# Eighteen late steps behind the last slots instead of twelve, the late halves' additions among them, the last half summed in a bank of its own

## The chip, the cores and the metric

The kernel runs on one core of a Trainium2 chip. The metric is the device time of one execution in microseconds (us), taken as the median of a few runs. PE is TensorE (matmuls), ACT is ScalarE, DVE is VectorE, POOL is GpSimd and SP is SyncE, which here only issues DMAs. Each engine works through its own instructions in order and waits on semaphores for the others.

## What is computed

8192 tokens (16 sequences of 512) with 128 features, all in float32. First a block per sequence: layer norms, a time mix with a scan along the sequence, a channel mix. Then a layer with one expert out of 16 for each token and a shared expert for all:

```python
x = x + attn(layernorm(x))                # time mix (scan) and channel mix
hidden = layernorm(x).reshape(-1, 128)
logits = hidden @ router_w.T              # 16 experts, the best one is taken
routed_out = einsum(up * silu(gate), down_proj)      # of the token's expert, EF = 128
shared = (silu(hidden @ shared_gate_w.T) * (hidden @ shared_up_w.T)) @ shared_down_w.T   # SF = 512
out = x + shared + expert_sum
```

## The kernel before

The program has two parts. In 23 rounds (`ROUNDS`) the 16 sequences run through the first block in a software pipeline; each token's row (its features for the expert, its own number, and the sum so far) is then scattered to a place in DRAM (`sorted_rows`) where the tokens of one expert lie together. The second part takes these sorted rows in 80 slots of 128 tokens, two slots (a pair) at a time: 40 pairs (`NP`), in 43 turns (`TURNS`). `one_turn(m)` stands in the program of each engine. In turn m

- SP has loaded pair k long before, from `sorted_rows` into a ring of 12 buffers (L392), once the scatter of pair k-12 is done
- PE transposes the features of pairs m and m+1 when m is even (L691), and DVE copies them out (L1133)
- PE does the down products of pair m-3 (L697) and the gate and up products of pair m-1 (L704, L705)
- ACT copies the weights of the two slots' experts (L865) and takes Silu of the gate product (L870); DVE multiplies it with the up product (L1141) and adds the down product to the rows (L1136)
- POOL scatters the two slots' rows to `out` (L1287), each token to its own place

The shared expert is not finished for all tokens in the first part. A sequence has two halves of 256 tokens; 16 halves are late (`LATE`, units u = 0 to 15). Units 0 to 2 are worked out in the last rounds, the others (`FIRST_LATE` = 3 and up) in late steps put between the slots. A unit has four steps. Steps 0 and 1 are its gate and up products (`unit_product`, L418: 4 matmuls, 8 records in the profile), ACT's Silu (L735) and DVE's product (L1124). Steps 2 and 3 are its down products (`unit_down_late`, L426: 4 matmuls, 8 records each) into bank 0 (`ACC`), which ACT copies out to `sh_of(u)` after step 3 (L738). `late_order` weaves two units: (u, 0), (u-1, 2), (u, 1), (u-1, 3). All gate products of the second part but the first two go to bank 2 and all up products to bank 3, so a gate product waits for the Silu before it and an up product for DVE's product before it; a down step waits for ACT's copy of the unit before.

`late_steps(m)` says which late steps stand in turn m: one each in turns 0 and 1, then 34 spread over turns 4 to 39 (`LATE_TURN` = 4), and the last 12 (`LATE_AFTER`) in the three turns that have no new pair: one in turn 40, one in turn 41 and the other ten in turn 42.

When all scatters are done (`all_stored`), SP and POOL load the late halves' rows back from `out` in 8 DMAs of two units each (`load_late`, L330; the places are `SP_LOADS` = 0, 2, 6, 8, 12, 14 and `GP_LOADS` = 4, 10). DVE then adds `sh_of(u)` to each unit (L1152), after all its other work, and the units are stored: 0 to 11 by SP, 12 to 15 (`ACT_STORES` = 4) by ACT, each when `tl_add` has counted it (`store_late`, L336).

Of the kernel before, what the change touches and what calls it, by code (L numbers as in the profile page):

```python
# [23 lines left out]
ALU = mybir.AluOpType  # L24
# [11 lines left out]
NT = NTOK // T  # L36
HALF = T // 2
# [55 lines left out]
def program(nc, x, w_main, w_exp, vecs, out):  # L93
# [4 lines left out]
    with ExitStack() as ctx:  # L98
# [124 lines left out]
        ACT_STORES = 4  # L223
        SP_LOADS, GP_LOADS = [u for u in range(0, N_LATE, 2) if u % 6 != 4], [u for u in range(0, N_LATE, 2) if u % 6 == 4]
        HALF_TILE = 10
# [3 lines left out]
        FIRST_LATE = len(C_TILES)  # L229
        STEPS_BEFORE, LATE_TURN, LATE_AFTER = 4, 4, 12  # L230
        GU_BEHIND, DN_BEHIND = 1, 3
# [65 lines left out]
        def stores(k):  # L297

            return range(2) if k < NP - 1 else range(1)

        def late_act(u):
            return actB if u % 2 else actC
# [7 lines left out]
        def tl_sem(u):  # L310

            if u - u % 2 in GP_LOADS:
                return "tl_in", 16 * (len(GP_LOADS) - 1)
            return f"xr_in{u // 2}", 32 * laps(u // 2)
# [85 lines left out]
        def _(pe):  # L400
# [52 lines left out]
            def late_step(u, step):  # L453
# [16 lines left out]
                else:  # L470
                    if u == FIRST_LATE:
                        wait(pe, "cbase", NT)
                    wait(pe, "lac", u, step - 1)
                    wait(pe, "lsh", u - 1)
                    unit_down_late(ACC, late_act(u)[step - 2], step - 2).then_inc(s["lD"], 1)

# [238 lines left out]
        def _(act_e):  # L715
# [12 lines left out]
            def late_step(u, step):  # L728
                if step < 2:
# [5 lines left out]
                    af(late_sg(u)[step][:, :], late_bank(u, step)[0][:, :], ACT.Silu).then_inc(s["lsg"], 1)  # L735
                elif step == 3:
                    wait(act_e, "lD", u)
                    af(sh_of(u), ACC[:, 0:HALF], ACT.Copy).then_inc(s["lsh"], 1)  # L738
# [141 lines left out]
        def _(dve):  # L880
# [235 lines left out]
            def late_step(u, step):  # L1116
                if step < 2:
# [6 lines left out]
                    v.tensor_tensor(late_act(u)[step][:, :], late_sg(u)[step][:, :], late_bank(u, step)[1][:, :], ALU.mult).then_inc(s["lac"], 1)  # L1124

            for u, step in late_order()[:STEPS_BEFORE]:
                late_step(u, step)

            def one_turn(m):
# [12 lines left out]
                for u, step in late_steps(m):  # L1142
                    late_step(u, step)

            for m in range(TURNS):
                one_turn(m)
            for u in range(N_LATE):
                if u % 2 == 0:
                    dve.wait_ge(s[tl_sem(u)[0]], tl_sem(u)[1] + 16)
                wait(dve, "cbase", NT)  # L1150
                wait(dve, "lsh", u)
                v.tensor_tensor(tl_of(u), tl_of(u), sh_of(u), ALU.add).then_inc(s["tl_add"], 1)  # L1152

# [179 lines left out]
```

## Time and profile before

| | |
|---|---|
| median of 3 timed runs | 510.09 us (509.06 to 510.21) |
| span of the profiled execution, first to last instruction | 528.1 us |
| TensorE busy | 497.9 us (94%) |
| VectorE busy | 363.4 us (69%) |
| ScalarE busy | 345.9 us (66%) |
| GpSimd busy | 347.9 us (66%) |
| the second part's first scatter | at 380.20 us |
| late halves' loads are issued | from 513.08 us |
| last late step's matmuls end | at 521.35 us |
| last addition ends | at 524.72 us |

All times of the trace are from the profiled execution, whose span is longer than the timed runs; of the profiled execution no other time is recorded than this span. Times in a row are microseconds from the start of the span, unless marked ns. PE's rows are records: one float32 matmul leaves two. Buffers are named by the tile they were made as: the slots use buffers of the first part again, so `er`, `e`, `num` and others in a row are their names there. The names `xn1tok`, `xn1T`, `ew` and `kr` in a row of L738 or L1152 are the late units 0 to 3, 4 to 7, 8 to 11 and 12 to 15 (`sh_of`).

### The profile page before, as it was taken

Reading aid. Unit: us, or ns where it says so; the run is one execution under the profiler, and the core shown is the slowest. Engines: PE = TensorE matmul, PEld = TensorE weight load, DVE = VectorE, ACT = ScalarE, POOL = GpSimd, SP = SyncE. Lnnn points to the kernel's source line nnn. Section 1 sums busy time; section 2 is a strip of 40 time slices with the busy share of each in tenths; the row PEclk is TensorE's granted clock in tenths of the full one; section 3 lists DMA queues with packets and bytes.
Section 4 is the critical chain, followed back from the end, with each engine's and each line's share of the span. In section 5 each row is a group of like instructions: output and inputs, shape, how many; then the busy total and the mean of one; then the engine's idle time right before and its main releaser. Section 6 shows DMA issues by size and latency. Waiting matters only on the chain.

```text
span 528.1 us, 10518 instructions
## 1 busy us (share of the span) xinstructions
PE 497.9 (94%) x3101; PEld 406.0 (77%) x3101; DVE 363.4 (69%) x1036; ACT 345.9 (66%) x643; POOL 347.9 (66%) x576
## 2 busy tenths in 40 slices
PE   8889999999999999999999999999998998799984
PEld 7646777877877877878577679888887987799874
DVE  5978889889889889888787888446434433444335
ACT  3777897987987988977789775632534534455321
POOL 6766668778778778785887866635154565556660
PEclk9999999999999999999999999999999899999988
DMA  6015001101101101101010010102877434441009
GB/s 219 2 51 209 20 21 41 60 22 41 60 21 42 60 22 42 50 11 62 12 50 21 21 41 32 41 21 72 204 207 189 137 101 125 129 116 49 30 12 308
DMA packets 33031, 39.32 MB, mean 74 GB/s; under 512 B 4913, under 2 KB 29113, under 8 KB 32720
## 3 DMA queue, kind: packets, MB, share of 16 engines
q1 hardware_dynamic: 26640, 24.97, 16.2%
q0 software_dynamic: 5760, 13.16, 7.2%
q8 instruction: 26, 0.43, 0.3%
q10 hardware_dynamic: 576, 0.52, 0.3%
q14 instruction: 29, 0.24, 0.2%
HBM read 21.68 MB, written 17.93 MB: 75 GB/s over the span
## 4 chain that ended last, share of the span: by engine, by line
PE 61%; DVE 7%; ACT 7%; issue 7%; another core or an unknown queue 7%; POOL 6%; DMA 2%; SPq 1%; ACTq 0%; DVEq 0%; POOLq 0%
PE bank L418 14%; PE bank L411 8%; PE bank L435 4%; PE bank L405 3%; PE bank L426 3%; PE bank L704 2%; PE bank L705 2%; PE bank L534 2%; PE bank L520 2%; PE bank L544 2%; PE bank L530 2%; PE bank L525 2%; PE bank L551 2%; PE bank L577 2%
## 5 line engine op out<-in xcount | busy, mean ns | idle before, releaser
L418 PE MATMUL bank<-hT,wm 128*128 128x256 f32 x512 | 128.7, 390 | 3.4 <-ACT hT L821 2.2
L418 PEld LDWEIGHTS bank<-hT,wm 128*128 128x128 f32 x512 | 94.0, 195 | 21.8 <-ACT hT L821 7.2
L1287 POOL DMA_INDIRECT out<-shared x55 | 53.9, 979 | 47.3 <-DVE shared L1136 32.2
L411 PEld LDWEIGHTS bank<-wm,k 128*128 128x128 f32 x512 | 62.3, 192 | 10.7 <-issue 6.9
L411 PE MATMUL bank<-wm,k 128*128 128x128 f32 x512 | 63.7, 277 | 1.2 <-ACT k L838 0.9
L870 ACT ACTIVATE er<-bank 128x256 f32<-128x256 f32 x40 | 15.2, 383 | 54.9 <-remote 33.1
L1141 DVE TENSOR_TENSOR e<-er,bank 128x256 f32<-128x256 f32 x40 | 16.8, 420 | 31.1 <-ACT er L870 20.3
L1287 POOL DMA_INDIRECT out<-rows x24 | 23.5, 978 | 20.5 <-DVE rows L1136 11.3
L799 ACT ACTIVATE h<-rows,smE 128x128 f32<-128x128 f32 x64 | 26.3, 482 | 12.6 <-POOL smE L1231 12.5
L435 PE MATMUL bank<-wm,actA 128*128 128x128 f32 x240 | 32.8, 280 | 0.0
L435 PEld LDWEIGHTS bank<-wm,actA 128*128 128x128 f32 x240 | 29.3, 192 | 0.2
L1245 POOL TENSOR_SCALAR shared<-shared,smA 128x128 f32<-128x128 f32 x64 | 27.8, 445 | 0.0
L761 ACT ACTIVATE xn1tok<-shared,smA 128x128 f32<-128x128 f32 x62 | 25.4, 482 | 3.2 <-POOL smA L1199 3.2
L1207 POOL TENSOR_TENSOR smA<-smA,half 128x8 f32<-128x8 f32 x15 | 25.7, 1716 | 1.2
L766 ACT ACTIVATE xn2T<-bank,vec 128x512 f32<-128x512 f32 x16 | 12.4, 777 | 20.4 <-PE bank L405 20.2
L1222 POOL TENSOR_SCALAR rows<-h,sc 128x128 f32<-128x128 f32 x64 | 24.1, 393 | 1.6
L1182 POOL TENSOR_SCALAR smC<-mvC 128x4 f32<-128x4 f32 x16 | 3.9, 244 | 30.8 <-DVE mvC L901 30.8
L896 DVE BATCH_NORM_STATS2 stA<-shared 128x6 f32<-128x128 f32 x64 | 13.9, 279 | 14.2 <-DMA shared<-x 14.2
L1258 POOL DMA_INDIRECT sorted_rows<-rows,posi x16 | 18.7, 1170 | 7.4 <-DVE posi L973 3.9
L534 PEld LDWEIGHTS bank<-wm,xn2T 128*128 128x128 f32 x128 | 16.8, 192 | 7.6 <-issue 7.6
L1264 POOL DMA_INDIRECT sorted_rows<-rows,posi x16 | 18.0, 1123 | 4.9 <-issue 4.9
L426 PE MATMUL bank<-wm,den 128*128 128x128 f32 x144 | 20.3, 289 | 0.5 <-issue 0.5
(258 smaller groups left out, 1401.6 us busy)
## 6 DMA issues: line engine op xcount, KB each, us to landing
shared<-sorted_rows SPq DMA_DIRECT2D x56, 128.5 KB
shared<-x SPq DMA_DIRECT2D x16, 256.0 KB
rows<-sorted_rows SPq DMA_DIRECT2D x24, 128.5 KB
wexp<-w_exp SPq DMA_DIRECT2D x2, 1536.0 KB, 9.6
sorted_rows<-filler SPq DMA_DIRECT2D x17, 128.5 KB
shared<-out SPq DMA_DIRECT2D x6, 256.0 KB
out<-shared SPq DMA_DIRECT2D x12, 128.0 KB, 2.3
sorted_rows<-rows,posi POOLq DMA_INDIRECT x64
```

The lines of the kernel that those rows point to most:

```text
L411: ins = mm(grp(acc, g), grp(lhs, g), W(name, f), start=(f == 0 and g == 0), stop=(f == F // P - 1), skip_group_check=True)
L418: ins = mm(dst[:, j * HALF:(j + 1) * HALF], W(name, 2 * pair_ + j), src[:, half * HALF:(half + 1) * HALF], start=True, stop=True)
L426: ins = mm(grp(acc, g), lhs[:, j * HALF + g:(j + 1) * HALF:2], W("down", 2 * pair_ + j), start=(pair_ == 0 and j == 0 and g == 0), stop=(p ...
L435: ins = mm(grp(acc, 2 * half + g), lhs[:, at_:at_ + P], W("down", 2 * pair_ + j), start=(pair_ == 0 and j == 0 and g == 0), stop=(pair_ == ...
L534: ins = mm(grp(REC_B, g), grp(xn2T[t % 2], g), W("Wrec"), start=True, stop=True)
L761: ins = af(grp(xn1tok[t % 2], g), grp(xin[t % XR], g), ACT.Identity, bias=smA[t % 3][:, 5, g:g + 1], scale=smA[t % 3][:, 4, g:g + 1])
L799: ins = af(grp(h[t % 2], g), base_of(t)[:, g, :], ACT.Identity, bias=smE[t % 3][:, 3, g:g + 1], scale=smE[t % 3][:, 1, g:g + 1])
L1207: g_.tensor_tensor(sm[:, 3:5, :], sm[:, 1:3, :], half8[:, :, :], ALU.pow).then_inc(s["pA"], 1)
L1222: ins = g_.tensor_scalar(rows[t % 3][:, g, 0:D], grp(h[t % 2], g), sc[t % 2][:, g:g + 1], 1.0, ALU.mult, ALU.mult)
L1245: ins = g_.tensor_scalar(grp(xn0[t % 4], g), grp(xin[t % XR], g), smA[t % 3][:, 0, g:g + 1], smA[t % 3][:, 3, g:g + 1], ALU.add, ALU.mult)
L1258: g_.indirect_dma_start(sorted_ap, bass.IndirectOffsetOnAxis(posi[t % 3][:, 2:3].bitcast(U32), 0), rows[t % 3][:, 2, :], None).then_inc(s[ ...
L1287: g_.indirect_dma_start(out, bass.IndirectOffsetOnAxis(xr[k % RING][:, j, D:D + 1].bitcast(U32), 0), xr[k % RING][:, j, D + 1:ROW], None, ...
```

## The change

Six more late steps are taken from the turns with slots and put into turn 42 (`LATE_AFTER` 18 instead of 12): 28 instead of 34 are spread over turns 4 to 39. The additions of units 0 to 13 are moved between DVE's last late products: units 0 to 3 behind the product of (14, 1), 4 to 7 behind (15, 0), 8 to 13 behind (15, 1). The last unit's down products go to bank 6 (`late_sum`), which the slots' transposes used; ACT does not copy them, and DVE adds the bank directly. SP loads pairs 0, 2, 4, 6, 8, 14 and POOL 10, 12.

```diff
--- before.py
+++ after.py
@@ -221,13 +221,14 @@
 
         TAB_ROWS = 15
         ACT_STORES = 4
-        SP_LOADS, GP_LOADS = [u for u in range(0, N_LATE, 2) if u % 6 != 4], [u for u in range(0, N_LATE, 2) if u % 6 == 4]
+        SP_LOADS, GP_LOADS = [0, 2, 4, 6, 8, 14], [10, 12]
+        ADDED_BEHIND = {(N_LATE - 2, 1): range(0, 4), (N_LATE - 1, 0): range(4, 8), (N_LATE - 1, 1): range(8, N_LATE - 2)}
         HALF_TILE = 10
         WARM_FIRST, WARM_BEFORE, WARM_BEHIND = 20, (8, 12), 4
         FULL_SLOTS = NTOK // P - NE
         FILL_PAIRS = range(4, 4 + NE)
         FIRST_LATE = len(C_TILES)
-        STEPS_BEFORE, LATE_TURN, LATE_AFTER = 4, 4, 12
+        STEPS_BEFORE, LATE_TURN, LATE_AFTER = 4, 4, 18
         GU_BEHIND, DN_BEHIND = 1, 3
         W_BEHIND = GU_BEHIND - 1
         TURNS = NP + DN_BEHIND
@@ -298,6 +299,10 @@
 
             return range(2) if k < NP - 1 else range(1)
 
+        def late_sum(u):
+
+            return bank[6] if u == N_LATE - 1 else ACC
+
         def late_act(u):
             return actB if u % 2 else actC
 
@@ -309,7 +314,7 @@
 
         def tl_sem(u):
 
-            if u - u % 2 in GP_LOADS:
+            if u // 2 * 2 in GP_LOADS:
                 return "tl_in", 16 * (len(GP_LOADS) - 1)
             return f"xr_in{u // 2}", 32 * laps(u // 2)
 
@@ -471,8 +476,11 @@
                     if u == FIRST_LATE:
                         wait(pe, "cbase", NT)
                     wait(pe, "lac", u, step - 1)
-                    wait(pe, "lsh", u - 1)
-                    unit_down_late(ACC, late_act(u)[step - 2], step - 2).then_inc(s["lD"], 1)
+                    if u == N_LATE - 1:
+                        wait(pe, "xhT", NP // 2 - 1)
+                    else:
+                        wait(pe, "lsh", u - 1)
+                    unit_down_late(late_sum(u), late_act(u)[step - 2], step - 2).then_inc(s["lD"], 1)
 
             def one_round(n):
                 at = at_round(n)
@@ -733,7 +741,7 @@
                         wait(act_e, f"cac{step}", NT)
                         wait(act_e, f"hac{step}", NT)
                     af(late_sg(u)[step][:, :], late_bank(u, step)[0][:, :], ACT.Silu).then_inc(s["lsg"], 1)
-                elif step == 3:
+                elif step == 3 and u < N_LATE - 1:
                     wait(act_e, "lD", u)
                     af(sh_of(u), ACC[:, 0:HALF], ACT.Copy).then_inc(s["lsh"], 1)
 
@@ -1123,6 +1131,18 @@
                         wait(dve, f"hD{step}", NT)
                     v.tensor_tensor(late_act(u)[step][:, :], late_sg(u)[step][:, :], late_bank(u, step)[1][:, :], ALU.mult).then_inc(s["lac"], 1)
 
+            def add_late(units):
+                for u in units:
+                    if u % 2 == 0:
+                        dve.wait_ge(s[tl_sem(u)[0]], tl_sem(u)[1] + 16)
+                    if u == N_LATE - 1:
+                        wait(dve, "lD", u)
+                        v.tensor_tensor(tl_of(u), tl_of(u), late_sum(u)[:, 0:HALF], ALU.add).then_inc(s["tl_add"], 1)
+                    else:
+                        wait(dve, "cbase", NT)
+                        wait(dve, "lsh", u)
+                        v.tensor_tensor(tl_of(u), tl_of(u), sh_of(u), ALU.add).then_inc(s["tl_add"], 1)
+
             for u, step in late_order()[:STEPS_BEFORE]:
                 late_step(u, step)
 
@@ -1141,15 +1161,11 @@
                     v.tensor_tensor(xact[k % 4][:, :], xsg[k % 2][:, :], XGU_B[k % 2][:, 2 * P:4 * P], ALU.mult).then_inc(s["xact"], 1)
                 for u, step in late_steps(m):
                     late_step(u, step)
+                    add_late(ADDED_BEHIND.get((u, step), ()))
 
             for m in range(TURNS):
                 one_turn(m)
-            for u in range(N_LATE):
-                if u % 2 == 0:
-                    dve.wait_ge(s[tl_sem(u)[0]], tl_sem(u)[1] + 16)
-                wait(dve, "cbase", NT)
-                wait(dve, "lsh", u)
-                v.tensor_tensor(tl_of(u), tl_of(u), sh_of(u), ALU.add).then_inc(s["tl_add"], 1)
+            add_late(range(N_LATE - 2, N_LATE))
 
 
         @block.gpsimd
```

PE, from turn 39 to the first steps of turn 42, before. L697 are down products of slots, L704 and L705 their gate and up products, L418 and L426 the late steps of the two kinds:

```order
L697 MATMUL bank<-an,e 128x128 x2
...
L697 MATMUL bank<-xn2T,e 128x128 x2
L704 MATMUL bank<-num,rv 128x128
L705 MATMUL bank<-num,rv 128x128
L418 MATMUL bank<-hT,wm 128x256 x4
L697 MATMUL bank<-th,e 128x128 x2
L426 MATMUL bank<-wm,den 128x128 x4
L697 MATMUL bank<-rv,e 128x128
L418 MATMUL bank<-hT,wm 128x256 x4
L426 MATMUL bank<-wm,actB 128x128 x4
```

The same place now (L705 is the down product of slots, L712 and L713 gate and up, L423 and L431 the late steps), with the start of what follows:

```order
L705 MATMUL bank<-an,e 128x128 x2
...
L705 MATMUL bank<-xn2T,e 128x128 x2
L712 MATMUL bank<-num,rv 128x128
L713 MATMUL bank<-num,rv 128x128
L423 MATMUL bank<-hT,wm 128x256 x4
L705 MATMUL bank<-th,e 128x128 x2
L431 MATMUL bank<-wm,actB 128x128 x4
L705 MATMUL bank<-rv,e 128x128
L423 MATMUL bank<-hT,wm 128x256 x4
L431 MATMUL bank<-wm,actB 128x128 x4
L423 MATMUL bank<-hT,wm 128x256 x4
L431 MATMUL bank<-wm,den 128x128 x4
```

The turns read alike, but behind the last slot's down product (`rv,e` with a single matmul) stand 16 late steps now, where ten stood.

DVE behind the last slots, before. L1136 adds a slot pair's down product, L1124 is a late product, L1152 an addition to the late halves:

```order
L1136 TENSOR_TENSOR shared<-bank,shared 128x2x128 x2
L1124 TENSOR_TENSOR den<-ev,bank 128x512 x2
L1124 TENSOR_TENSOR actB<-sgB,bank 128x512 x2
L1152 TENSOR_TENSOR shared<-shared,xn1tok 128x256 x4
L1152 TENSOR_TENSOR shared<-shared,xn1T 128x256 x4
L1152 TENSOR_TENSOR shared<-shared,ew 128x256 x4
L1152 TENSOR_TENSOR shared<-shared,kr 128x256 x4
```

And now (L1132 is a late product, L1144 an addition, L1140 the addition that reads the bank):

```order
L1132 TENSOR_TENSOR den<-ev,bank 128x512
L1132 TENSOR_TENSOR actB<-sgB,bank 128x512 x2
L1132 TENSOR_TENSOR den<-ev,bank 128x512 x2
L1144 TENSOR_TENSOR shared<-shared,xn1tok 128x256 x4
L1132 TENSOR_TENSOR actB<-sgB,bank 128x512
L1144 TENSOR_TENSOR shared<-shared,xn1T 128x256 x4
L1132 TENSOR_TENSOR actB<-sgB,bank 128x512
L1144 TENSOR_TENSOR shared<-shared,ew 128x256 x4
L1144 TENSOR_TENSOR shared<-shared,kr 128x256 x3
L1140 TENSOR_TENSOR shared<-shared,bank 128x256
```

Eight additions stand ahead of the last late product, and eight behind it.

## Rows read from the trace of the kernel before

**Rows 1.** The page's first line: span of the profiled execution.
```profile
span 528.1 us, 10518 instructions
```
**Rows 2.** Windows of 4 us: busy times, granted clock, DMA share, GB/s.
```profile
504.00:508.00 4.00, 4.00 (x19) 3.65 (x18) 1.62 (x4) 0.38 (x1) 3.08 (x4) 0.57 0.02 0
...
520.00:524.00 4.00, 1.34 (x12) 1.15 (x10) 3.40 (x11) 0.38 (x1) 0.00 (x0) 1.00 1.03 349
```
**Rows 3.** Chain of waits, an undisturbed stretch: start, duration, what.
```profile
476.40 0.44 PE bank L691 x4
...
478.18 0.94 PE bank L426 x8
...
480.46 1.73 PE bank L418 x8
482.19 0.44 PE bank L691 x4
```
**Rows 4.** The chain's unrecorded waits: first and last of eight.
```profile
390.21 5.46 another core or an unknown queue
...
498.15 4.59 another core or an unknown queue
```
**Rows 5.** Timeline of POOL: start, duration, operation, idle time before it and releaser.
```profile
440.87 0.98 POOL L1287 DMA_INDIRECT out<-shared  x1 [3.03 <-DVE shared L1136]
442.15 0.98 POOL L1287 DMA_INDIRECT out<-shared  x1 [0.30 <-issue]
...
450.68 0.98 POOL L1287 DMA_INDIRECT out<-rows  x1 [2.41 <-DVE rows L1136]
```
**Rows 6.** Timelines of PE: turn 4's transposes, and turns 39 to 42.
```profile
379.36 0.38 PE L691 MATMUL bank<-ident,shared 128*128 128x128 f32 x2
...
497.55 0.61 PE L697 MATMUL bank<-an,e 128*128 128x128 f32 x4
...
498.89 0.61 PE L697 MATMUL bank<-xn2T,e 128*128 128x128 f32 x4
...
503.65 0.71 PE L697 MATMUL bank<-th,e 128*128 128x128 f32 x4 [1.97 <-DVE e L1141]
504.20 1.73 PE L426 MATMUL bank<-wm,den 128*128 128x128 f32 x8
505.72 0.64 PE L697 MATMUL bank<-rv,e 128*128 128x128 f32 x2
```
**Rows 7.** Timeline of all engines behind the last slot.
```profile
506.15 2.73 PE L418 MATMUL bank<-hT,wm 128*128 128x256 f32 x8
...
508.72 1.10 PE L426 MATMUL bank<-wm,actB 128*128 128x128 f32 x8
...
513.08 3.15 SPq L330 DMA_DIRECT2D shared<-out  x6
...
513.92 1.13 PE L418 MATMUL bank<-hT,wm 128*128 128x256 f32 x4 [0.47 <-DVE den L1124]
...
517.81 0.69 DVE L1124 TENSOR_TENSOR actB<-sgB,bank 128x512 f32<-128x512 f32 x1 [1.98 <-PE bank L418]
518.42 1.43 DVE L1152 TENSOR_TENSOR shared<-shared,xn1tok 128x256 f32<-128x256 f32 x4
...
519.22 2.12 PE L426 MATMUL bank<-wm,actB 128*128 128x128 f32 x16 [0.56 <-ACT kr L738]
520.60 1.43 DVE L1152 TENSOR_TENSOR shared<-shared,xn1T 128x256 f32<-128x256 f32 x4 [0.75 <-DMA shared<-out]
...
523.29 1.43 DVE L1152 TENSOR_TENSOR shared<-shared,kr 128x256 f32<-128x256 f32 x4
```
**Rows 8.** Stores by source line (ns; starts), groups by line, DMA issues (landing).
```profile
L336 ACTq DMA_DIRECT2D out<-shared x4: 412/461/591, 523.7 to 525.2; - x4
...
L1136 DVE TENSOR_TENSOR shared<-bank,shared 128x256 f32<-128x256 f32 x26 | 10.9, 419 | 10.8 <-PE bank L697 5.5 <-remote 4.9 <-issue 0.3
...
shared<-out POOLq DMA_DIRECT2D x2, 256.0 KB, 5.6
```

## The prediction

> **What bounds the kernel now.** I read the page's first line and set it beside the times [rows 1]: the profiled execution's span is 528.1 us, the median of the timed runs 510.09 us, so the profiled execution is 18.0 us or more behind a timed one, and the reader has to ask where. The change lies in the last quarter, so next came the chain of waits. In an undisturbed stretch [rows 3] it is TensorE (PE) alone: from one x4 transpose to the next, two turns, are 476.40 to 482.19 = 5.79 us. Those two turns hold 0.44 us of transposes, twice 1.34 of down, gate and up products (the step from one down product to the next in a turn without a late step, 497.55 to 498.89 in [rows 6]) and two late steps, 0.94 and 1.73: 5.79 us, with nothing between them. So a turn costs PE 1.56 us for its pair of slots and 2.90 us with a late step (1.34 on average). GpSimd (POOL) issues the two scatters of a turn 1.28 us apart [rows 5], 2.57 us a turn, so it is not the bound.
>
> The same chain has eight pieces that end in no recorded work [rows 4], 35.8 us together, the first at 390.21, the last from 498.15 to 502.74. In each, VectorE (DVE) and ScalarE (ACT) stand still although PE's records say that their product is done. From the transposes of turn 4 at 379.36 to the last slot's down product at 505.72 [rows 6] are 126.4 us. The work in it is 38 turns x 1.56 = 59.3 and 36 late steps x 1.34 = 48.1, together 107.4 us: 19.0 us are lost. That is nearly the 18.0 us by which the profiled execution is long. I conclude that most of this loss belongs to the profiled execution and that in a timed run the slots go at PE's pace. This is an inference from two numbers, and the main rival hangs on it.
>
> The Trainium skill, page "Runtime: NRT & Kernel Launch", section "The ~15µs preamble/postamble breakdown", puts 9 to 15 us around a kernel's own instructions; by it a timed run's span would be 495 to 501 us and the surplus of the profiled one 27 to 33 us. No row here shows that part. It would make the slots of a timed run still more surely PE's, with the same sum.
>
> Behind the slots [rows 6, 7] PE does ten late steps, 506.15 to 521.35 us. Their work is 4 x 1.73 + 6 x 0.94 = 12.6 us; the rest is a stretch at the lower clock [rows 2] and two gaps of 0.47 and 0.56 us. DVE, which has to do all 16 additions after its last product at 517.81, starts them at 518.42 and ends at 524.72. The last store leaves at 525.2 and the span ends 2.9 us later [rows 7, 8]. So what ends the kernel is DVE's block of additions and not PE, which is done 3.4 us before it.
>
> **The change, part by part.**
>
> Six late steps leave the slots, three of each kind (34 between turns 4 and 39 become 28): 3 x 1.73 + 3 x 0.94 = 8.0 us of PE. Where the turns are PE's, the last slot is done 8.0 us sooner: 36 turns at 1.56 + 28 x 1.34 / 36 = 2.60 us on average instead of 1.56 + 34 x 1.34 / 36 = 2.83. Bounds of what is given back: 8.0 us, and 0. A turn without a late step stands in the trace, from the down product at 497.55 to the next at 498.89 [rows 6]: 1.34 us, what the undisturbed stretch holds too, no gap. So I take 8.0 us.
>
> The same six steps are added behind the last slot: +8.0 us of PE. One bank pair (2 and 3) takes all gate and up products there, so a stall can sit between steps. Before, two gaps did, 0.47 us before 513.92 and 0.56 us before 519.22 [rows 7]. Per six steps I add 0.5 us, the first gap once; bounds 0 and 1.5.
>
> The last half sums in bank 6. The second gap is PE waiting for ACT to empty bank 0 (the releaser in the row at 519.22); with its own bank the last unit needs only DVE's product, done at 518.50, and starts behind the step before it, at 518.66. PE ends 0.56 us sooner, at 520.8 on the old clock. ACT's last copy (0.38 us) goes; the addition reads the bank itself, at the price of an addition with a bank operand, 0.42 us [rows 8].
>
> Of the additions, units 0 to 3 go behind the product of (14, 1), 4 to 7 behind (15, 0), 8 to 13 behind (15, 1). Four take 1.43 us and one 0.42, so each starts (1.43 - 0.42) / 3 = 0.34 us after the one before [rows 7, 8]. Four of them with a product are 0.69 + 1.43 = 2.1 us, and PE needs 0.94 + 1.73 = 2.67 us until its next up product: they fit, 0.5 us to spare. Behind the last product remain eight instead of 16: from 518.42 the six end at 520.5, unit 14 at 520.9, and unit 15, which waits for PE at 520.8, at 521.25, where 524.72 stood. ACT's stores of units 12 to 15 go out from 520.25 at one every 0.5 us, the last at 521.8 instead of 525.2. So the end comes 3.4 us sooner in the profiled execution. Of that, 0.75 us is DVE's wait for a load [rows 7], which a timed run, whose scatters lag less behind, may not have: for the timed run I take 3.0 (2.6 to 3.5).
>
> What the moved additions wait for: in order on DVE, the product of (15, 0) and with it PE's up product of (15, 1) are queued behind the landing of pairs 0 and 2. Before, loads were issued 7.4 us after the last slot's down product (505.72 to 513.08), and the slowest took 5.6 us to land [rows 6 to 8]: 13.0 us. Now (14, 1) ends five gate and four down steps after that point, 5 x 1.73 + 4 x 0.94 = 12.4 us and the gaps; pairs 0 and 2 are the first two of SP's queue and land before the slowest. Pairs 4 and 6 are wanted 2.7 us later, 8 to 13 another 2.7 us later. SP takes pair 4 from POOL and gives it 12; each issue is 0.46 us. All that is covered, narrowly for the first two in the worst case.
>
> Traffic: loads and stores are 4.2 MB. Before, they ran at 349 GB/s from 520 to 524 us, the DMA engines busy throughout [rows 2]; at that rate 4.2 MB are 12 us. Now the loads have 12 us to themselves and only 1 MB of stores is left for the last 3 us.
>
> Sum on the profiled execution: -8.0 + 8.0 + 0.5 - 3.4 = -2.9, a span of 525.2 us. On a timed run: -8.0 + 8.0 + 0.5 - 3.0 = -2.5, so **507.6 us**.
>
> **The rivals.**
>
> A, slower: the slots are not PE's in a timed run. If the eight unrecorded waits are real there and come at a pace that PE's work does not set (the scatters go in sixes, and the next six starts about 10 us after, 440.87 and 450.68 [rows 5]), fewer steps in a turn only lengthen them. Then up to 8.0 us is not given back: 510.09 + 8.0 + 0.5 - 3.0 = 515.6. It decides where less than 8.0 - 2.5 = 5.5 us of the 8.0 are given back. For it: eight such waits. Against: 19.0 against 18.0 us. 17 in 100; it may be partial, about 511.5.
>
> B, no change: 1 to 4 us of the 8.0 are lost. POOL's 79 scatter intervals need 79 x 1.28 = 101.3 us, and PE's slots would fall to 107.4 - 8.0 = 99.4 us: POOL becomes as slow as PE. That delays the loads, not PE, as long as the ring of 12 pairs does not fill. 509 to 510.5 us, 13 in 100.
>
> C, the lower clock behind the slots. The row: from 504 to 508 us the granted clock was 0.57, that is 1.2 GHz for most of it and 2.4 after, behind 1.97 us without a matmul [rows 2, 6]; the down step from 504.20 took 1.52 us to the next product instead of 0.94, the gate and up step from 506.15 to 508.72 2.57 instead of 1.73 [rows 3, 6, 7]: +1.4 us. More of PE's work now stands in that place and depends on ACT and DVE step by step. Once more gives 507.6 + 1.4 = 509.0 us, 7 in 100. The Trainium skill, page "TensorE: Matmul & The Clock Gate", section "HAM oscillation — how this bites in real kernels", has idle stretches between bursts return the array to the lower clock; by that rule this would come with every such gap. The gap of 0.56 us before 519.22 was followed by no fall (granted clock 1.00 from 520 to 524 [rows 2]), so the trace bears it out for the long gap only.
>
> D, the additions hold DVE back: pairs 0 and 2 land after (14, 1). Each us late is a us on the end; 0.5 to 2 us, 508 to 509.6. Against: 12.4 us of steps before they are wanted. 5 in 100, mostly no change.
>
> E, more: no stall behind the slots, the 3.4 us of the profile whole, and a second effect of less work per turn: 505.0 to 506.6, 10 in 100.
>
> **How the numbers follow.** The forecast (507.6, itself 506.6 to 508.6) has 48 in 100, E 10. With the parts of C and D below 508.56 that makes faster 0.62. Within 0.3% (about 1.5 us, what a measurement of this kernel can tell from no change) is 0.20: B, most of C and D, and the light part of A. Slower is 0.18: A with what is left. The range of 8 in 10 runs from E's lower end, 505.0, to the partial case of A, 511.5.
>
> **What would show it.** In the changed profile: two slot turns without an unrecorded wait near 5.2 us on average; 16 late steps in 20.6 us of work and at most 1.5 us of gaps after the last slot's down product; additions between the products with no DVE wait for a load before them; the last one, from bank 6, right behind PE's last matmul, and the span's end 3.3 us after it where it was 6.75 us. It would be wrong if the last slot's down product does not come about 8 us sooner in the profile, or if products of (15, 0) and (15, 1) start later than 1 us behind their up products.

## The result and the profile after

The changed kernel took **503.95 us** (median of 6 runs, 503.52 to 507.69), the kernel before 509.97 us beside it (6 runs, 509.06 to 510.48). The ratio is 0.9888, with an interval of 0.9862 to 0.9913: 6.0 us faster, where 2.5 were forecast. The sign was right, the size was not, and 503.95 lies 1 us under the range of 505.0 to 511.5.

The page of the changed kernel, its span and its busy times:

```profile
span 504.8 us, 10516 instructions
...
PE 488.0 (97%) x3101; PEld 400.4 (79%) x3101; DVE 363.0 (72%) x1036; ACT 348.6 (69%) x642; POOL 348.9 (69%) x576
```

[rows 1] had 528.1 us in that place, 18 us over the timed median. The profiled execution of the changed kernel took 506.53 us, 1.7 us more than its span. So a profiled execution is not long as such, and the first question was what the 528.1 us had been.

The timeline of the changed kernel, PE behind and around the last slot (start, duration, operation), and SP's loads:

```profile
480.48 0.39 PE L705 MATMUL bank<-rv,e 128*128 128x128 f32 x2
480.70 1.89 PE L423 MATMUL bank<-hT,wm 128*128 128x256 f32 x8
...
487.71 3.15 SPq L335 DMA_DIRECT2D shared<-out  x6
...
499.34 2.05 PE L431 MATMUL bank<-wm,actB 128*128 128x128 f32 x16
```

The last slot's down product starts at 480.48, the transposes of turn 4 at 382.44: the slots take 98.0 us. PE's last matmul ends at 499.34 + 2.05 = 501.39, 20.9 us behind the last down product. From there to the span's end are 3.4 us.

The timeline of DVE and of ACT's stores in the changed kernel, with the idle time before each and its releaser:

```profile
493.34 0.69 DVE L1132 TENSOR_TENSOR den<-ev,bank 128x512 f32<-128x512 f32 x1 [1.97 <-PE bank L423]
493.94 1.42 DVE L1144 TENSOR_TENSOR shared<-shared,xn1tok 128x256 f32<-128x256 f32 x4
...
496.61 1.42 DVE L1144 TENSOR_TENSOR shared<-shared,xn1T 128x256 f32<-128x256 f32 x4
...
499.27 1.42 DVE L1144 TENSOR_TENSOR shared<-shared,ew 128x256 f32<-128x256 f32 x4
500.61 1.08 DVE L1144 TENSOR_TENSOR shared<-shared,kr 128x256 f32<-128x256 f32 x3
501.06 1.89 ACTq L341 DMA_DIRECT2D out<-shared  x4
501.62 0.41 DVE L1140 TENSOR_TENSOR shared<-shared,bank 128x256 f32<-128x256 f32 x1
```

No addition waits for a load, and the last one, from bank 6, starts 0.23 us behind PE's last matmul. All this is close to what the prediction drew. What it got wrong is therefore looked for in the kernel before, against which the change is set.

### The profile page after: what moved, and what is told of

The parts are those of the page before. It is cut to its first block and busy times, and to the rows that moved or that the text cites. A ratio compares the mean times of both kernels' runs of the same rounds, so it can differ in the third digit from the quotient of the medians.

```text
span 504.8 us, 10516 instructions
## 1 busy us (share of the span) xinstructions
PE 488.0 (97%) x3101; PEld 400.4 (79%) x3101; DVE 363.0 (72%) x1036; ACT 348.6 (69%) x642; POOL 348.9 (69%) x576
## 5 line engine op out<-in xcount | busy, mean ns | idle before, releaser
L423 PE MATMUL bank<-hT,wm 128*128 128x256 f32 x512 | 125.5, 384 | 4.6 <-ACT hT L829 4.4
L423 PEld LDWEIGHTS bank<-hT,wm 128*128 128x128 f32 x512 | 91.6, 190 | 22.5 <-ACT hT L829 10.5
L1274 POOL DMA_INDIRECT sorted_rows<-rows,posi x16 | 18.7, 1170 | 7.4 <-DVE posi L981 3.1
L985 DVE TENSOR_TENSOR ew<-bank,ew 128x512 f32<-128x512 f32 x16 | 11.0, 687 | 17.8 <-ACT ew L815 11.6
L904 DVE BATCH_NORM_STATS2 stA<-shared 128x6 f32<-128x128 f32 x64 | 13.9, 280 | 12.4 <-DMA shared<-x 12.4
L774 ACT ACTIVATE xn2T<-bank,vec 128x512 f32<-128x512 f32 x16 | 12.4, 778 | 14.3 <-PE bank L410 14.0
L1132 DVE TENSOR_TENSOR actB<-sgB,bank 128x512 f32<-128x512 f32 x14 | 9.6, 688 | 15.2 <-PE bank L423 11.5
```

Of the source, the lines that this page charges most:

```text
L423: ins = mm(dst[:, j * HALF:(j + 1) * HALF], W(name, 2 * pair_ + j), src[:, half * HALF:(half + 1) * HALF], start=True, stop=True)
L1274: g_.indirect_dma_start(sorted_ap, bass.IndirectOffsetOnAxis(posi[t % 3][:, 2:3].bitcast(U32), 0), rows[t % 3][:, 2, :], None).then_inc(s[ ...
```

## Experiments

Three theories. **P**: the slots lose 2 to 4 us in ordinary runs too, and a lighter turn wins them back. **Q**: the slots are PE's; the end of the kernel before costs more in ordinary runs than the first profile showed. **R**, formed after the second group: that end hangs on the scatters, the loads behind them and the stores, and not on PE. Each comparison below is with the kernel before on the same chip, with its interval of 95%.

### First group: a chip on which the kernel before takes 532 us

The kernel before, unchanged:

> The kernel before, unchanged, profiled once more. What is open: the change gained 6.0 us where 2.5 were forecast, while the changed kernel's profile shows the tail as forecast (3.4 us from TensorE's last matmul to the end). Theory P: in ordinary runs too the kernel before loses 2 to 4 us in its slots, to waits that end in no recorded work or to gaps of TensorE, and the change takes them away. Then this profile has a span near 508.3 us (the time less 1.7) and shows such waits, and its tail is the known 6.0 to 6.8 us behind TensorE's last matmul. Theory Q: the slots lose nothing in ordinary runs; the tail behind the last slot costs more there than in the first profile. Then TensorE is without a gap up to the last slot, and the tail is 9 us or more.

The kernel before with one number changed:

```diff
-STEPS_BEFORE, LATE_TURN, LATE_AFTER = 4, 4, 12
+STEPS_BEFORE, LATE_TURN, LATE_AFTER = 4, 4, 18
```

> The kernel before with one number changed: 18 late steps behind the last slots instead of 12. Additions all at the end, the last unit in bank 0, as before. P: the slots give back more than the 8.0 us moved, so this alone gains 2 to 4 us, 506 to 508 us. Q: 8.0 us out and 8.0 us in, with another 0 to 0.5 us of gaps: 510.0 to 510.5 us.

The changed kernel with `LATE_AFTER` back at 12, which leaves the early additions and the own bank:

> The changed kernel with 12 late steps behind the slots instead of 18: the additions between the products and the own bank alone. Now the product of (14, 1) comes some 5.3 us after the last slot's down product and the loads of pairs 0 and 2 land 8 to 10 us after it, so VectorE waits for them 3 to 5 us ahead of the product of (15, 0) and holds TensorE. P and Q alike: 3.4 us gained on the additions, 3 to 5 lost, 509.5 to 512 us. Under Q a gain larger than 3.4 us on the tail may show, 507 to 509 us.

The changed kernel with all of the additions but the last two behind the last product:

```diff
-ADDED_BEHIND = {(N_LATE - 2, 1): range(0, 4), (N_LATE - 1, 0): range(4, 8), (N_LATE - 1, 1): range(8, N_LATE - 2)}
+ADDED_BEHIND = {(N_LATE - 1, 1): range(0, N_LATE - 2)}
```

> The changed kernel with the additions of units 0 to 7 moved back behind the last late product: 18 steps, own bank and the new order of loads kept. Eight more additions of 0.34 us on VectorE's tail, 2.7 us: 503.95 + 2.7 = 506.7 us under both theories. If P is right, this lies 3 us below the kernel before for the move of the six steps; under Q it would have to be the early additions that bring the gain, and this would be 508 us or more.

Measured: the kernel before 532.0 us here (the median of all its runs on this chip is 532.33); the move alone 539.98, ratio 1.0155 (1.0102 to 1.0209); additions and bank with 12 steps 531.14, 0.9978 (0.9944 to 1.0013); additions at the end 538.18, 1.0108 (1.0069 to 1.0147). No theory had foreseen 532 us, and none of the expectations for the three edits came true: the timed runs here are as long as the first profile, and the move alone, for which 506 to 510.5 us were expected, is 7.7 us slower than before. Windows of 40 us in the slots (PE, PEld, DVE, ACT and POOL busy with their counts, granted clock, DMA share, GB/s), of the kernel before on this chip:

```profile
425.00:465.00 40.00, 34.76 (x232) 31.57 (x231) 14.82 (x32) 16.59 (x41) 22.20 (x24) 0.91 0.41 113
```

and of the kernel before on another chip (the profile of the second group, below):

```profile
425.00:465.00 40.00, 40.00 (x312) 38.54 (x311) 20.50 (x43) 22.44 (x55) 27.63 (x29) 1.00 0.49 138
```

The same stretch holds 232 of PE's matmuls against 312. The chain of waits of the long run shows where, in the same kind of piece as [rows 4]:

```profile
401.96 6.56 another core or an unknown queue
...
444.99 6.95 another core or an unknown queue
```

From the trace's semaphore events one can work out how long after the end of its record each of PE's updates in the slots arrives (the next update of that semaphore). In the first profile and in the six traces taken on the two chips of 532 and 535 us it is 2.4 to 2.8 us on average, over 1 us for 74 to 92 of 138 to 147; in the nine others it is 0.01 to 0.08 us, over 1 us for at most 2. (Some updates are missing from the long traces, so these averages are rough.) So on such a chip, a lagging one in what follows, the next engine gets PE's word late. Since the ends of PE's records are modelled, this does not tell whether the matmuls end late or only the update comes late. In all seven lagging traces the first update that is over 0.5 us late belongs to a matmul some 4 us behind the first indirect scatter of the program, and the last one within 3 us of the start of the last scatter; no run tested whether the scatters cause it.

The slots take 124.9 us in the kernel before and 129.5 with the move alone: six steps fewer in them, and nothing given back. That is rival A's mechanism. It can't be what made the change faster in the first comparison, so the same had to be asked on a chip without it.

### Second group: a chip on which the kernel before takes 510 us

The kernel before:

> The kernel before, unchanged, once more, on whatever chip this is. On the chip of the last four runs it took 532 us, and TensorE's semaphore updates came up to some microseconds behind its records in the slots. Where the chip takes 510 us for it: theory P says that 2 to 3 us of such lag are in the slots there too (more than 107.4 us from turn 4's transposes to the last slot's down product), theory Q that the slots take 106 to 107.5 us and the tail more than the 21 us of the first profile.

The changed kernel:

> The changed kernel, unchanged, beside the kernel before on this chip. If the chip is one where the kernel before takes 532 us, the six steps moved cost 8 us and the additions and the bank give 5 to 6 back: 2 to 4 us slower than before. If it is one where before takes 510 us: 504 us, as in the first comparison.

The move alone, with the edit of the first group:

> The kernel before with 18 late steps behind the slots, nothing else. On a chip with the lag: 8 us slower, as measured. On one without: P (the slots give back more than 8.0 us) 2 to 4 us faster than before; Q (they give back 8.0) within 0.5 us of before.

The changed kernel with the last half summed in bank 0 again, emptied by ACT:

```diff
-            return bank[6] if u == N_LATE - 1 else ACC
+            return ACC
...
-                    if u == N_LATE - 1:
-                        wait(pe, "xhT", NP // 2 - 1)
-                    else:
-                        wait(pe, "lsh", u - 1)
+                    wait(pe, "lsh", u - 1)
...
-                elif step == 3 and u < N_LATE - 1:
+                elif step == 3:
```

Its addition then reads the copy in SBUF, as the other fifteen do.

> The changed kernel with the last unit back in bank 0 and ScalarE's copy of it back, all else kept. Then the last down products wait for ScalarE's copy of unit 14, 0.56 us, and the last addition for another copy, 0.4 to 0.5 us: 0.9 to 1.1 us behind the changed kernel under both theories, on either kind of chip.

Measured: before 510.29 (0.9993, 0.9975 to 1.0011); the change 503.12 (0.9878, 0.9820 to 0.9935); the move alone 507.23, ratio 0.9934 (0.9910 to 0.9959), some 3 us; without the own bank 504.24, 504.38 and 505.40 us, ratio 0.9871 (0.9827 to 0.9915), which can't be told from the whole change by its times (a fourth run of it took 1293.72 us, for which nothing here gives a reason; it is left out). The move alone was expected within 0.5 us of before by Q and 2 to 4 us faster by P, so its time speaks for P; its stages do not. The stages of the traces, in us (the slots from turn 4's transposes to the last slot's down product; PE's tail from there to the end of its last matmul; the rest to the span's end):

| kernel | slots | PE's tail | rest | span |
|---|---|---|---|---|
| before, first profile | 126.4 | 15.6 | 6.8 | 528.1 |
| before, this chip | 106.1 | 13.7 | 9.3 | 509.0 |
| the change, first profile | 98.0 | 20.9 | 3.4 | 504.8 |
| the change, this chip | 98.1 | 20.9 | 3.4 | 500.8 |
| move alone | 98.6 | 21.7 | 6.3 | 506.4 |
| without the own bank | 98.7 | 21.7 | 3.7 | 503.7 |

The parts in front of the slots differ by up to 1.6 us between two traces of the same kernel, so the stages say more than the spans. The slots give back 8.0 us of 8.0 with the change and 7.5 with the move alone, none more than was moved: **P falls**. The tail takes 7.2 with the change and 8.0 with the move alone. The rest of 9.3 us in the kernel before is the surprise, 2.5 us more than in the first profile; the move alone makes it 3.0 us shorter, the change 5.9. The timeline of the kernel before on this chip, from the last slot on:

```profile
486.05 0.39 PE L697 MATMUL bank<-rv,e 128*128 128x128 f32 x2
...
491.04 0.98 POOL L1287 DMA_INDIRECT out<-shared  x1 [0.30 <-issue]
...
493.23 3.15 SPq L330 DMA_DIRECT2D shared<-out  x6
493.79 1.55 POOL L330 DMA_DIRECT2D shared<-out  x2 [1.77 <-DMA out<-shared]
...
496.25 0.69 DVE L1124 TENSOR_TENSOR actB<-sgB,bank 128x512 f32<-128x512 f32 x1 [1.97 <-PE bank L418]
496.86 1.43 DVE L1152 TENSOR_TENSOR shared<-shared,xn1tok 128x256 f32<-128x256 f32 x4
497.65 2.12 PE L426 MATMUL bank<-wm,actB 128*128 128x128 f32 x16 [0.56 <-ACT kr L738]
...
500.93 1.43 DVE L1152 TENSOR_TENSOR shared<-shared,xn1T 128x256 f32<-128x256 f32 x4 [2.65 <-DMA shared<-out]
502.28 1.42 DVE L1152 TENSOR_TENSOR shared<-shared,ew 128x256 f32<-128x256 f32 x4
503.62 1.43 DVE L1152 TENSOR_TENSOR shared<-shared,kr 128x256 f32<-128x256 f32 x4
504.07 2.08 ACTq L336 DMA_DIRECT2D out<-shared  x4
```

DVE stands 2.65 us before the second four additions, for POOL's loads; in [rows 7] it was 0.75. Both of POOL's loads count one semaphore (`tl_in`), and the addition of unit 4 waits for both: by the semaphore's updates pair 4 was there at 499.62 and pair 10 at 500.91, where the wait ends. A semaphore for each would have won little, since SP's pair 6, needed two additions later, came at 501.11. The loads leave at 493.23, 7.2 us after the last slot's down product (7.4 in the first profile), since the last scatter starts 5.0 us after it. But PE is done sooner: its tail is 13.7 us here against 15.6. So the loads are late for the additions. Their landing, by the DMA issues (count, KB each, median us):

```profile
shared<-out SPq DMA_DIRECT2D x6, 256.0 KB, 7.1
shared<-out POOLq DMA_DIRECT2D x2, 256.0 KB, 6.1
```

and the DMA engines' share (the last column but one) is full all the while:

```profile
496.00:500.00 4.00, 3.21 (x25) 2.86 (x23) 2.03 (x5) 0.57 (x2) 0.00 (x0) 1.00 0.90 283
500.00:504.00 4.00, 0.00 (x0) 0.00 (x0) 3.07 (x10) 0.20 (x1) 0.00 (x0) 1.00 1.01 348
504.00:508.00 4.00, 0.00 (x0) 0.00 (x0) 1.05 (x4) 0.00 (x0) 0.00 (x0) 0.60 0.88 294
```

From 493.2 to the end, 4.2 MB of loads and stores have to pass: that is theory R, tested in the third group.

The Trainium skill, page "DMA: Bandwidth & Descriptors", section "🔬 Latency and other measured facts", gives HBM's access 2 us at high load as the main part of a transfer's fixed cost. The 7.1 us here are mostly something else: the eight loads of 256 KB share full engines, and the same loads with a quarter of the bytes (below) landed 2.6 us after their issue. Reckoning with the page's figure alone would have had the additions never wait.

### Third group: what the end hangs on, on another such chip

The kernel before with loads of a quarter of the bytes:

```diff
-                eng.dma_start(shared[:, u * HALF:(u + 2) * HALF].rearrange("p (h c) -> p h c", h=2),
-                              halves_[:, a0:a1 + 1:a1 - a0, :]).then_inc(s[tl_sem(u)[0]], 16)
+                eng.dma_start(shared[:, u * HALF:(u + 2) * HALF].rearrange("p (h c) -> p h c", h=2)[:, :, 0:HALF // 4],
+                              halves_[:, a0:a1 + 1:a1 - a0, 0:HALF // 4]).then_inc(s[tl_sem(u)[0]], 16)
```

> The kernel before, but each late half's load brings a quarter of its columns (64 of 256), so that three quarters of the late halves' output is not the reference's; additions, stores and all else are kept. In the kernel before on an undisturbed chip the additions wait 2.65 us for a load, TensorE ends 9.27 us before the end, and the DMA engines are busy from the last scatter to the end. Theory R: there the end hangs on the scatters, the loads behind them and the stores, not on TensorE. Then this kernel loses the wait: additions from 0.6 us behind the last late product in one row, TensorE's end to the end 6.3 us, 507.3 us. Rival: the wait hides nothing and the end is where it was, 510 us. On a chip with the lag (532 us): 530 to 532 us.

The early additions and the own bank with 12 late steps behind, again:

> The changed kernel with 12 late steps behind the slots, for an undisturbed chip. The loads go out 7.1 us after the last slot's down product, the product of (14, 1) ends 5.5 us after it. R: VectorE waits for pairs 0 and 2, which land 3 to 4 us after their issue, so the product of (15, 0) is some 4 to 5 us late and TensorE's end with it, but the end hangs on the DMA traffic anyway: 13 us from the loads' issue, so 507 to 509.5 us. If the end hung on TensorE alone: 510.3 + 4.5 - 5.9 = 509 us, so only the trace tells these apart: under R the stores' DMA is busy to the end.

The changed kernel with `LATE_AFTER` at 24:

> The changed kernel with 24 late steps behind the slots instead of 18. With the loads landed well before the additions want them, nothing more is to be had: 503.1 us, within 0.5. TensorE's slots would be 90.5 us where GpSimd's 79 scatter intervals need 101.3, so GpSimd lags 10 us more; if that holds TensorE through the ring of 12, 504 to 506 us. On a chip with the lag: another 8 us slower.

The kernel before with pair 4 first on SP's queue and 12 on POOL's:

```diff
-SP_LOADS, GP_LOADS = [u for u in range(0, N_LATE, 2) if u % 6 != 4], [u for u in range(0, N_LATE, 2) if u % 6 == 4]
+SP_LOADS, GP_LOADS = [0, 2, 4, 6, 8, 14], [10, 12]
```

> The kernel before with the changed kernel's order of loads alone: pairs 0, 2, 4, 6, 8, 14 by SyncE, 10 and 12 by GpSimd. If what ends the kernel before is its additions waiting for pair 4 and 10 on GpSimd's queue, the wait of 2.65 us falls to 0 to 1 us and this gains 2 to 2.5 us, 508 us. If it is the 4.2 MB behind the last scatter (13 us at 320 GB/s), the order gives 0 to 1 us, 509.5 us.

Measured, beside 511.17 us for the kernel before:

| kernel | us | ratio (interval) | slots | PE's tail | rest |
|---|---|---|---|---|---|
| quarter loads | 507.52 | 0.9935 (0.9910 to 0.9961) | 106.3 | 13.7 | 6.3 |
| additions and bank, 12 steps | 510.39 | 0.9995 (0.9976 to 1.0013) | 105.8 | 18.6 | 4.6 |
| the change with 24 steps | 503.95 | 0.9863 (0.9839 to 0.9886) | 90.5 | 28.9 | 3.4 |
| order of the loads | 510.80 | 0.9989 (0.9973 to 1.0005) | 106.0 | 13.7 | 9.9 |

**Quarter loads.** Nothing but the loads' bytes is cut, and 3.65 us go, close to R's 507.3, with the rest at 6.3 us, just where the move alone has it. DVE's additions run through:

```profile
496.68 1.42 DVE L1152 TENSOR_TENSOR shared<-shared,xn1tok 128x256 f32<-128x256 f32 x4
498.02 1.42 DVE L1152 TENSOR_TENSOR shared<-shared,xn1T 128x256 f32<-128x256 f32 x4
```

The same two rows with the move alone, where six more steps stand behind the slots and the additions are as before:

```profile
497.21 1.42 DVE L1152 TENSOR_TENSOR shared<-shared,xn1tok 128x256 f32<-128x256 f32 x4
498.55 1.42 DVE L1152 TENSOR_TENSOR shared<-shared,xn1T 128x256 f32<-128x256 f32 x4
```

Two unlike edits take the same wait away and win some 3 us each, so R holds on chips without the lag. This is what the six moved steps are worth: from the start of the last scatter to the first addition are 13.8 us with the move alone and 5.8 before.

**Order of the loads.** The wait isn't POOL's queue being behind: with pair 4 third on SP's, it landed 7.6 us after its issue, DVE waited longer, and the time did not change. The loads share the DMA engines, and another place in the queues did not bring this one in sooner.

```profile
502.06 1.50 DVE L1152 TENSOR_TENSOR shared<-shared,xn1T 128x256 f32<-128x256 f32 x4 [3.48 <-DMA shared<-out]
```

**Additions and bank with 12 steps.** This is rival D's mechanism in full. The timeline of DVE and PE:

```profile
495.93 1.52 DVE L1144 TENSOR_TENSOR shared<-shared,xn1tok 128x256 f32<-128x256 f32 x4 [4.39 <-DMA shared<-out]
497.37 0.68 DVE L1132 TENSOR_TENSOR actB<-sgB,bank 128x512 f32<-128x512 f32 x1
...
498.20 1.14 PE L423 MATMUL bank<-hT,wm 128*128 128x256 f32 x4 [2.97 <-DVE actB L1132]
499.13 1.91 PE L431 MATMUL bank<-wm,den 128*128 128x128 f32 x8
...
501.30 1.43 DVE L1144 TENSOR_TENSOR shared<-shared,xn1T 128x256 f32<-128x256 f32 x4 [3.25 <-DMA shared<-out]
```

DVE waits 4.39 us for the loads with PE's next input queued behind, and PE stands 2.97 us. The tail is 4.9 us longer than before, the rest 4.7 us shorter: nothing won, where R had let expect 507 to 509.5 us. The early additions pay only once the move has made time for the loads.

It also shows rival C's price. Windows of the same kernel:

```profile
498.00:502.00 4.00, 3.80 (x18) 3.74 (x19) 0.75 (x4) 0.39 (x1) 0.00 (x0) 0.64 0.93 302
```

After the 2.97 us without a matmul the granted clock is 0.64 in this window, mostly 1.2 GHz where it had been 2.4, and the down step of eight matmuls at 499.13 took 1.91 us instead of 1.10. After the 0.56 us gap of the kernel before, the window 496 to 500 above has 1.00. The Trainium skill, page "TensorE: Matmul & The Clock Gate", section "HAM oscillation — how this bites in real kernels", has waits for a DMA between bursts of matmuls bring the lower clock back. The trace agrees for the gap of 2.97 us, behind which stands DVE's wait for a load; the gap of 0.56 us, a wait for ACT's copy, had no such effect.

**24 steps.** Twelve steps moved instead of six: 503.95 us, ratio 0.9863 against 0.9878 for the change in the second group, intervals that overlap; 503.1 within 0.5 had been expected. The slots give back another 7.6 us and the tail takes 8.0. So POOL's scatters do not bound slots of 98 us (rival B), and once the loads are ahead more room for them brings nothing.

### Fourth group: a lagging chip again

The changed kernel with the additions at the end, and the changed kernel:

> The changed kernel with the additions of units 0 to 7 moved back behind the last late product; 18 steps, own bank and order of loads kept. On an undisturbed chip the loads have landed before the first addition, so only eight additions of 0.34 us are added to the tail: 2.7 us behind the changed kernel, 505.9 us, 4.4 us faster than before. On a chip with the lag of TensorE's semaphore updates: again 1% slower than before.

> The changed kernel unchanged on one more chip. Undisturbed (before 510 to 511 us): 503 to 504 us. With the lag (before 530 us or more): the steps moved cost 8 us, as the move alone did (7.7), and the tail gives back 2.7 us for the early additions more than the kernel with all additions at the end, which was 5.9 us slower than before: 3 us slower than before.

Measured beside 535.0 us for the kernel before: 542.0, ratio 1.0147 (1.0067 to 1.0227), and 537.45, ratio 1.0040 (1.0008 to 1.0071). On such a chip the change is **slower**, by some 2 us, where 3 had been expected. The stages of the lagging traces, with the time of the traced run:

| kernel | run | slots | PE's tail | rest |
|---|---|---|---|---|
| before, first profile | not recorded | 126.4 | 15.6 | 6.8 |
| before | 535.6 | 124.9 | 21.0 | 6.3 |
| additions and bank, 12 steps | 529.9 | 121.7 | 21.9 | 4.3 |
| move alone | 540.8 | 129.5 | 21.7 | 6.3 |
| additions at the end, first group | 540.1 | 126.5 | 24.9 | 7.1 |
| additions at the end, this group | 540.8 | 127.4 | 23.6 | 7.1 |
| the change | 542.5 | 128.3 | 28.8 | 3.4 |

With 34 late steps the slots took 121.7 to 126.4 us, with 28 of them 126.5 to 129.5: no trace shows any of the 8.0 us given back, and the slots are 3.6 us longer on average. The granted clock is not the main thing missing. In the window below, of the move alone on the first lagging chip, it is 1.00, and yet 244 matmuls are done where the same kernel does 313 on a chip without the lag:

```profile
425.00:465.00 40.00, 33.14 (x244) 29.95 (x243) 15.80 (x34) 17.65 (x44) 22.93 (x24) 1.00 0.41 120
```

The early additions shorten the rest from 7.1 to 3.4 us here. The medians of the last two kernels are 4.5 us apart, with intervals wide enough for the 2.7 that was expected. The change's trace is of its longest run, 5 us over its median, so its tail of 28.8 us says little of the others.

## Why the prediction was wrong

**The surplus of 18 us** was taken for something that profiled executions add. In kind that was wrong: it belongs to the chip on which that profile was taken, or to one like it; on two chips the timed runs are that long too. The first profile's updates lag like those of the long runs. The conclusion that was drawn from it, that on the chips of 510 us the slots go at PE's pace, was right, but not for its reason: the same kernel on a lagging chip loses about as much in timed runs too, and that the change was timed on a chip without the lag was luck.

**−8.0 in the slots.** Right: 106.1 to 98.1 us, where 107.4 to 99.4 were forecast. In the changed kernel's windows of the slots PE is busy without a pause:

```profile
420.00:440.00 20.00, 20.00 (x158) 19.33 (x157) 10.36 (x23) 12.28 (x29) 15.19 (x16) 1.00 0.52 151
```

**+8.0 behind them.** Right: the move alone has a tail of 21.7 us against 13.7.

**+0.5 of gaps.** Did not come: those 8.0 us are the steps themselves. The stall at 513.92 in [rows 7] is not in the tail of a chip without the lag, and neither is the lower clock. Step by step the first profile's tail loses 0.84 us at that stall (0.47 of them the gap) and 1.05 to the clock; 15.6 less these is 13.7. (The prediction's 1.4 us for the clock holds 0.58 from before the tail.)

**−0.56 from the own bank.** Right in kind and near in size: PE's tail is 20.9 us with it and 21.7 without, and the rest 3.4 against 3.7, together 1.1 us by one pair of traces.

**−3.0 for the additions: the step that failed.** The prediction had 3.4 us in the profile, took off up to 0.75 for DVE's wait for a load "which a timed run, whose scatters lag less behind, may not have", and so took 3.0. It is the other way round. The loads are issued just as late (7.2 us after the last down product, 7.4 in the first profile), while PE's tail, the thing that covers them, is 1.9 us shorter, and the wait is 1.9 us longer: 2.65 us. That tail could have been reckoned from the prediction's own rows, since the gap of 0.47 us and the lower clock stood in them as effects of the waits.

The 3.0 counts to the end of the kernel and holds the 0.56 of the own bank. Measured in the same way the term is 6.7 us: 0.8 from the tail, 5.9 from the rest (9.3 to 3.4). The move alone brings 3.0 of them (9.3 to 6.3), nearly all of it DVE's wait; the prediction gave the move no gain at all, and the loads' lead of 8 us stood in it as a condition (12.4 us of steps against 13.0 us to the slowest landing) and not as a term. The early additions with the own bank bring the other 3.7. One us of these is a second thing that the prediction held fixed, at 2.9 us from the last store to the end: ACT has issued its last store 2.9 us before the end in the kernel before (504.07 + 2.08 of 509.0) and with the move alone, and 1.9 us before it with the change (501.06 + 1.89 of 504.8), where half of the 16 stores went out before the last late product. That the stores ahead of it make the difference is argued, not tested.

The sum with the measured terms: −8.0 + 7.2 − 5.9 = −6.7 us of stages, and 6.0 and 7.2 us in the two timed comparisons on chips without the lag. Of the 4.2 us between −2.5 and −6.7, 0.5 are the gaps that did not come, 2.3 the load wait beyond the 0.35 that the 3.0 still held of it, 1.0 the last store, and 0.4 lie within what two traces differ by. The prediction's sign "the span's end 3.3 us after it" came near the measured 3.4 by luck: its own figures give 521.8 + 2.9 − 520.8 = 3.9.

**The rivals.** A is real, on lagging chips: there it decides, and turns the change into +2 us, where the prediction had reckoned +5.5 at the worst. Two of the four chips of the later runs were lagging ones, so 17 in 100 was low for a mechanism that the only trace at hand showed eight times. B is refuted by 24 steps. C and D are both seen in the kernel with 12 steps, and both absent from the change on a chip without the lag, as was argued. E, "the 3.4 us of the profile whole, and a second effect", was the nearest, and its floor of 505.0 still too high.

**Time around the span.** The figure of 9 to 15 us that the prediction cited from the Trainium skill, page "Runtime: NRT & Kernel Launch", is not in these times: time less span is 1.7 us in the runs compared. Had the 1.7 us been read off, the surplus of the first profile would have been reckoned against a span of 508.4 us, 19.7 us, still near the 19.0 lost in the slots.

**What stays open.** Why PE's updates come late on some chips was not tried. The change's +2 us on a lagging chip are not divided by stages: the only trace of it there is of a run far from its median. The move alone cost 7.7 us there, and additions and bank with 12 steps won what can't be told from nothing (ratio 0.9978). The long tails there come from late updates too, which go on until the scatters are done: in the two traces with the additions at the end PE stands 3.2 and 2.4 us for ACT and DVE early in the tail, and in three others (the kernel before, additions and bank, the change) it works at a granted clock of 0.50 for some 4 us after such a stand as well. How much of this falls into the tail of a typical run is not shown.

## What to carry to other kernels

When a profile is longer than the timed runs, don't carry its waits over or strike them out one by one: a wait for a transfer is the difference of two clocks, the engine's and the DMA's, and if only the engine gets faster the wait grows. Work moved behind a phase of scatters is worth what it gives the loads that follow them, and early consumers pay only once that lead exists. Cutting the bytes of the suspected transfers in one run tells whether an end hangs on those transfers or on the engine that is busiest in front of it.

## What the runs showed of the hardware

The same kernel takes 510 to 511 us on some chips and 532 to 535 on others. In the long runs PE's semaphore updates arrive 2.4 to 2.8 us behind the ends of its records on average in the slots, from the first indirect scatter to the last, and the waiting engines show pieces of up to 7 us with no releaser. There the slots took 121.7 to 126.4 us with 34 late steps and 126.5 to 129.5 with 28. A change of 6 us for the better on one chip was 2 us for the worse on the other, so a result that rests on how full an engine's phase is should be taken on both kinds.

Eight loads of 256 KB issued within 3 us landed 7.1 us after their issue (median of SyncE's six), at DMA engines 0.9 to 1.0 busy and 283 to 348 GB/s with the stores; with 64 KB each it was 2.6 us. A stand of 2.97 us without a matmul was followed by a granted clock of 0.64 over 4 us, one of 0.56 us by none.
